# Neighbour rows of the masked activation: six VectorE copies or two DMAs of the sync engine

## The reference

```python
out1 = conv2d(x, conv2_w, conv2_b, PAD)
mask = sigmoid(conv2d(x, mask_w, mask_b, PAD))
xm = x * mask
q = conv2d(xm, q_w, q_b, 0)
pad_x = pad(xm, ((0, 0), (0, 0), (PAD, PAD), (PAD, PAD)))
k = conv2d(pad_x, k_w, k_b, 0)
v = conv2d(pad_x, v_w, v_b, 0)
sims = [sum(q * k[:, :, i:i + H, j:j + W], axis=1) for i in range(3) for j in range(3)]
attn = softmax(stack(sims, axis=-1), axis=-1)
out2 = sum over the 9 shifts of attn * v shifted
return out1 * mask + (1.0 - mask) * out2
```

## Time and profile before

| | us |
|---|---|
| median of 3 runs | 258.87 (258.56 to 259.05) |
| the profiled execution, own time | 257.9 |
| its span | 256.4 |
| PE busy | 182.8 (71%) |
| VectorE busy | 192.4 (75%) |
| ScalarE busy | 129.3 (50%) |
| GpSimd busy | 76.1 (30%) |
| chain that ended last | VectorE 43%, PE 36%, ScalarE 8%, issue 7% |

### The profile page before, as it was taken

How to read it: one execution, slowest core, us unless ns; L and a number is a source line. 1 busy time by engine, 2 the same in 40 slices (tenths; PEclk the granted TensorE clock), 3 DMA queues, 4 the chain that set the end, 5 groups by cost and what they waited for, 6 DMA issues and landing times.

```text
span 256.4 us, 4585 instructions
## 1 busy us (share of the span) xinstructions
PE 182.8 (71%) x1738; PEld 111.0 (43%) x1738; DVE 192.4 (75%) x426; ACT 129.3 (50%) x256; POOL 76.1 (30%) x56
## 2 busy tenths in 40 slices
PE   0508749897568957966998589976179977297763
PEld 0308529343146536434584448442034534146632
DVE  5498694883998999996979956549999348883552
ACT  2043161641675845566745563267545467514750
POOL 4754804031008026400182231000917100302341
PEclk9999997999889999995899957999659999867995
DMA  6311021000030000000002000000010000000101
GB/s 196 75 25 36 4 61 41 0 3 0 1 102 3 1 0 3 0 23 0 3 0 84 1 1 3 0 0 3 0 41 4 0 0 4 0 0 3 45 0 43
DMA packets 5190, 5.17 MB, mean 20 GB/s; under 512 B 3184, under 2 KB 3408, under 8 KB 5168
## 3 DMA queue, kind: packets, MB, share of 16 engines
q1 hardware_dynamic: 4928, 4.29, 5.9%
q10 hardware_dynamic: 240, 0.58, 0.8%
HBM read 3.30 MB, written 1.05 MB: 17 GB/s over the span
## 4 chain that ended last, share of the span: by engine, by line
DVE 43%; PE 36%; ACT 8%; issue 7%; DMA 3%; POOL 1%; SPq 1%; ACTq 0%; DVEq 0%
PE ps L1224 12%; DVE sh_in L283 6%; PE ps L1171 5%; PE ps L1260 5%; DVE sh_ln L298 3%; DVE sh_ln L283 3%; DMA w3b<-in_w_gi 3%; ACT sh_x L483 2%; PE ps L1151 2%; DVE ln_out L764 2%; PE ps L1232 2%; DVE sh_x L283 2%; PE ps L1316 2%; PE ps L1300 2%; DVE gi L866 2%
## 5 line engine op out<-in xcount | busy, mean ns | idle before, releaser
L392 POOL TENSOR_TENSOR ln_s<-ln_s,neg_half 128x16 f32<-128x16 f32 x8 | 23.4, 2924 | 98.5 <-DVE ln_s L747 98.5
L1224 PE MATMUL ps<-sh_ln,w_gi 96*128 96x512 f32 x96 | 42.4, 596 | 0.5 <-DVE sm L822 0.5
L483 ACT ACTIVATE sh_ln<-ln_out 32x512 f32<-32x512 f32 (+1 forms) x44 | 27.4, 622 | 22.0 <-DVE ln_out L772 15.3
L1171 PE MATMUL ps<-w_qk,sh_ln 128*128 128x128 f32 x192 | 26.6, 302 | 12.8 <-ACT sh_ln L483 12.8
L1260 PE MATMUL ps<-sh_in,w_in 128*32 128x256 f32 x384 | 26.2, 432 | 11.4 <-DVE sh_in L283 11.4
L1171 PEld LDWEIGHTS ps<-w_qk,sh_ln 128*128 128x128 f32 x192 | 25.4, 216 | 16.4 <-issue 16.4
L1224 PEld LDWEIGHTS ps<-sh_ln,w_gi 96*128 96x128 f32 x96 | 17.9, 190 | 22.1 <-issue 21.9
L1260 PEld LDWEIGHTS ps<-sh_in,w_in 128*32 128x32 f32 x384 | 13.0, 124 | 23.3 <-DVE sh_in L283 12.5
L866 DVE TENSOR_TENSOR gi<-ps,gate 64x512 f32<-64x512 f32 x16 | 11.1, 694 | 15.0 <-ACT gate L518 14.7
L518 ACT ACTIVATE gate<-ps 64x512 f32<-64x512 f32 x16 | 9.3, 587 | 20.2 <-PE ps L1224 20.2
L283 DVE COPY sh_in<-act_c 32x496 f32<-32x496 f32 (+1 forms) x28 | 17.2, 614 | 0.5
(11 more groups left out here) (129 smaller groups left out, 358.5 us busy)
## 6 DMA issues: line engine op xcount, KB each, us to landing
x_norm<-in_x SPq DMA_DIRECT2D x4, 256.0 KB, 2.7
x_res<-in_x SPq DMA_DIRECT2D x4, 256.0 KB, 2.5
out_x<-out_s SPq DMA_DIRECT2D x4, 256.0 KB, 2.0
sh_ln<-ln_out SPq DMA_DIRECT2D x8, 64.0 KB, 2.1
kc<-in_shape_consts ACTq DMA_DIRECT2D x1, 450.0 KB, 6.6
w3b<-in_w_gi SPq DMA_DIRECT2D x1, 288.0 KB, 6.5
vec<-in_vectors SPq DMA_DIRECT2D x1, 131.5 KB, 3.3
w3a<-in_w_qkv ACTq DMA_DIRECT2D x1, 108.0 KB, 3.2
```

Source lines behind the costliest of these rows:

```text
L392: nc.gpsimd.tensor_tensor(ln_s[n][:, 3, :], ln_s[n][:, 2, :], neg_half[:, :], ALU.pow)\
L483: return nc.scalar.activation(o, i, ACT.Copy)
L1171: mm = nc.tensor.matmul(to, sh_ln1[:, d, i, WD * y:WD * y + P], w_qk[:, dy, :, :, :].rearrange("p d m c -> p (d m c)"), start=(dy == 0), s ...
L1224: mm = nc.tensor.matmul(ps[:, GI_BANKS[2 * i + h], :], w_gi[:, dy, :, :].rearrange("p m o -> p (m o)"), xs[:, i, y:y + H // 2, 0:W], start ...
```

## The change

The six copies leave VectorE. The sync engine issues two DMAs for each pair instead, each over 96 partitions: one fills row 0 of partitions 32 to 127 from row 8 of partitions 0 to 95, the other row 9 of partitions 0 to 95 from row 1 of partitions 32 to 127. The signal now counts 32 for a pair, 16 for each DMA.

```diff
-        g_halo = signal("halo_copied", 1)
+        g_halo = signal("halo_copied", 32)
+            def halo(pair):
+
+                alone(sp)
+                sp.wait_ge(g_xm.sem, g_xm.done(pair))
+                sp.dma_start(xm[C:P, :, 0, :], xm[0:P - C, :, RH, :]).then_inc(g_halo.sem, 16)
+                sp.dma_start(xm[0:P - C, :, RH + 1, :], xm[C:P, :, 1, :]).then_inc(g_halo.sem, 16)
+
...
                 load_res(pair + 2)
+                halo(pair)
                 if norm:
                     ln1_planes(pair + 3)
                 store(pair)
...
             but_last, last = PAIRS - 2, PAIRS - 1
+            halo(but_last)
+            halo(last)
             store(but_last)
             store(last)
...
-                dve.wait_ge(g_xm.sem, g_xm.at(pair, 2))
-                for r in range(R - 1):
-                    nc.vector.tensor_copy(xm[C * r + C:C * r + 2 * C, :, 0, :], xm[C * r:C * r + C, :, RH, :])
-                    ins = nc.vector.tensor_copy(xm[C * r:C * r + C, :, RH + 1, :],
-                                                xm[C * r + C:C * r + 2 * C, :, 1, :])
-                ins.then_inc(g_halo.sem, 1)
```

## The result

The first four executions of the changed kernel had a median of 257.01 us (254.54 to 259.71), four of the kernel before 258.96 us (258.56 to 259.19). The ratio on record is 0.984, 95% interval [0.982, 0.986], and 0.983 and 0.988 in two later repetitions; each leaves out the executions that took over 1.5% longer than the fastest one of the same kernel. That first interval is too narrow. Over the whole study the kernel before gave 253.6 to 263.4 us and the changed kernel 250.9 to 259.7. Over all these executions the means are 257.7 us (55 of them) and 255.4 us (16). The difference is **-2.3 us, 95% interval [-3.8, -0.8]**, a ratio of 0.991 [0.985, 0.997]. The forecast was 2.9 us less. The change makes the kernel faster by about 1%, and the forecast lies inside the interval; by a threshold of 2% the two kernels would count as the same.

A forecast was written before the change was run, and what follows sets the result against it. VectorE was taken to bound pair 0, with k's and q's paths level in pair 1. Terms 2.4 + 0.87 - 0.4 = 2.9 us less: 258.87 - 2.9 = 256.0 us, 8-in-10 range 253.2 to 259.0.

The forecast's parts named there:

- SP's wait: On SP's queue in all four pairs: the new DMAs wait behind no other work, so no cost.
- How late the rows come: Neighbour rows in pairs 0 and 1: there 2.8 us after `xm` ends instead of 2.2, so 0.6 us later.
- The bound of 3.7 us: Slow limit for the landing of the new DMAs, if their 136-byte runs land as w_bd's did; 2.1 us was taken.
- VectorE in pair 0: Removing 2.15 us of copies in pair 0 saves 1.45 us, as L834 behind them inherits the wait for GpSimd.
- The second slowing: Later in pair 0, L736 escapes GpSimd's L419: 0.9 us won, 2.4 us at L989 with the 1.45 before it.
- To the end of the step: End of pair 0's step: the 2.4 us pass through, and L1232's matmul group at the high clock gives 0.87 us more.
- the further 0.87 us: Gain at the matmul group L1232 in pair 0, expected to run at the high clock; bounds 0 and 0.87.
- Pair 1: Scores in pair 1 wait for k and start at 151.2 instead of 150.78: a loss of 0.4 us, bounds 0 and 2.0.
- this high clock: Rival, chance 0.07: PE's clock stays high over pair 1's scores and v, 4.1 us more won, 251.9 us.
- Pairs 2 and 3: In pairs 2 and 3 PE comes to k late behind other work, so nothing is won or lost.
- the cap by PE in part 4: Limit on the gain at L989 in pair 0, set by when PE has the second score bank ready: 3.1 us.
- The rival of the fallen clock: Rival, chance 0.12: PE's clock falls in pair 0, leaving 0.5 us won there; 257.9 us in all.

The follow-up runs named there:

- e11: The changed kernel with GpSimd's first residual operation held back until `out1` is there in pairs 0 and 1; mean 255.5 us.
- e5: The changed kernel with three extra matmuls of unused result on PE in the steps of pairs 0 and 1; mean 254.4 us.
- e10: The changed kernel with the DMAs in pair 0 only and VectorE's copies back in pairs 1 to 3; mean 255.9 us.
- e1: The changed kernel run again without any edit; mean 254.5 us over six executions.
- e3: The kernel before with the six copies left out and nothing in their place, readers waiting for `xm` alone; mean 253.0 us.
- e2: The kernel before run again without any edit; mean 257.7 us.
- e6: The kernel before with three extra matmuls of unused result on PE in the steps of pairs 0 and 1; mean 258.5 us.
- e4: The changed kernel with the six copies back on VectorE, written into a tile that nobody reads; mean 257.3 us.

## Why the prediction was right or wrong

The median on record is 257.01 us against a forecast of 256.0; over all executions the change brought 2.3 us [0.8, 3.8] against 2.9. By its steps:

1. SP's wait: right. The DMAs were issued 0.07 to 0.10 us behind `xm`.
2. How late the rows come: right. An issue takes 0.61 us, a landing 1.9 us (2.1 assumed), and k started 2.72 us behind the end of `xm` (2.9 with the 0.1 for PE). The bound of 3.7 us was far off. The Trainium skill (DMA: Bandwidth & Descriptors, "Why small descriptors are slow (HBM only)") says that copies from SBUF to SBUF don't suffer the loss of short runs; the trace agrees, with 1.9 us for runs of 136 bytes against 2.1 for L333's longer ones.
3. VectorE in pair 0: right, 1.63 us at q for 1.45; L844, with two inputs in SBUF, inherited the wait and L842, with one, did not, as the Trainium skill (SBUF — State Buffer, "Who interferes with whom") has it. e11 shows that the wait was for GpSimd.
4. The second slowing: right where PE's clock did not fall before k. L746 escapes, L749 doesn't, and L993 comes 7.6 (e5, e10) to 7.8 us (e1) behind the end of `xm` for 7.7. In the other two profiles of the changed kernel k came so late that L749 escaped as well, and L993 waited for PE instead and came at 9.05 us. At the reduction 2.47 us for 2.4, where the clock was high (e5, e10).
5. To the end of the step: wrong. VectorE's gain did come through to the reduction, but the further 0.87 us were not the change's. The kernel before had the short 5.09 us from reduction to convolution too, in its second profile, with PE standing 2.70 us; and e3 had the long 5.95 us, though VectorE was 2.05 us sooner. What differs is the clock while that group runs: low in the first profile and in e3, high in the others. "v's matmuls start no later than before" was wrong in pair 1: the key windows are now last, and scores to `gate_info` take 4.77 us instead of 4.52 at the same clock.
6. Pair 1: the term was right for the case it assumed. It took the low clock over from the one trace before; at that clock the scores come 0.41 us later, as forecast (7.19 for 6.78, e11). At the high clock, which three of three profiles of the changed kernel had there, the scores start 5.97 us behind `xm` and the sign turns: 0.81 us won, 0.25 lost to the key windows. The prediction gave this high clock 0.07 and took it for a gain of the change; but the kernel before had it as well in its second profile.
7. Pairs 2 and 3: right. k starts 5.7 us behind `xm` in pair 3 where it was 5.5 and 5.7.

Two small slips in its arithmetic change nothing: the cap by PE in part 4 comes to 102.8 - 99.6 = 3.2 us and not 3.1, and the store of pair 0 is issued 8 us ahead of the end of pair 1's `xm`, not 7.

**The step that failed** is how PE's clock was treated: as a property of the program at each place, read from one execution, with 0.12 for a fall in pair 0. In all three profiles of the changed kernel it fell there; there pair 0 gave 0.75 us or lost 0.55, where the same work gave 2.47 at the high clock. In the kernel before the clock fell in pair 0 too, for a shorter time (e2, e6), and the reduction came no later. So the change has no one value: at the high clock throughout it brings 2.5 + 0.6 us, with a fall at k in pair 0 that part is 0.5 us behind a kernel before without such a fall. The rival of the fallen clock was therefore the right mechanism with too small a chance and a price a little too good (it had 0.5 won). What decides in which execution the clock falls is left open; no run sets it. The size was in part luck. The sum was 2.4 + 0.87 - 0.4 = 2.9; at the high clock the traces show 2.5 + 0 + 0.6 = 3.1, so two wrong terms nearly cancelled, and the mean over executions with and without falls came out near it too. The range held also because it had been made wide for these cases.

What is shown and what is argued: that the copies were on the bounding chain is shown by e3 (4.7 us less without them, 2.05 us of it ahead of pair 0's reduction) and by e4's marks (with them back 26.17 us to the reduction, against 24.5 without at the high clock). That a low clock takes pair 0's gain is shown by the marks: 24.3 to 24.5 us to the reduction in all six profiles that have the DMAs in pair 0, no copies there and a high clock, against 26.2 and 27.5 with 6.8 and 10.2 us at the low one. Whether the change makes the clock fall more often is not shown.

The 0.2% "that a measurement can tell" was wrong as well. Three executions within 0.2% said little about the spread, and a mean over six is uncertain by 2 us or more.

## What to carry to other kernels

When an engine's work is taken off the bounding chain, look for what its lateness had been covering: here VectorE's lateness could hide about 2.7 us of delay on PE, such as a fallen clock makes, and once most of it was gone the gain depended on the clock. Before a term is credited to the change, look for a second profile of the kernel before that shows it too: the 0.87 us at the reduction were in one. Read a stage by distances between marks in several traces before believing a difference of whole times, and don't take three close times for a small spread. A latency added to one path can pay elsewhere: the later k moved GpSimd away from one VectorE operation (L736, 1.16 us in e3 and 0.69 in e5), worth 0.4 us.

## What the runs showed of the hardware that I had not expected

- One program on one core, in the same study, spread by 10 us in 258 (253.6 to 263.4). Its mean granted clock went with it, but loosely: 0.915 in an execution of 255.9 us and 0.889 in that of 263.4, yet 0.896 in one of 255.6 and 0.914 in one of 259.5. Where the clock falls counts too: 3.4 us at the low clock cost 0.87 us when they began at the reduction (e3) and nothing there when they began 1.3 us behind it (e6).
- PE's clock fell to 0.50 behind stands of only 0.7 and 1.31 us with matmuls between them (changed kernel, 97.3), while another execution with the same stands kept 1.00 (e11, pair 0).
- Two small DMAs started together from two queues land in 2.2 to 2.3 us on SP instead of 1.9.
- An operation on 8 elements a partition waited 0.67 us for GpSimd, and it has two inputs in SBUF; the reciprocal before it, with one, did not wait.
